# Expert stages in three chunks of groups inside one block, with tiles of 128 places

## Time and profile before

| what | value |
|---|---|
| median of 3 runs | 2091.97 us (2087.68 to 2100.49) |
| the profiled execution | 2083.64 us, span 2081.6 us |
| mean granted TensorE clock | 0.909 of 2.4 GHz |
| busy share of the span | PE 83%, PE weight loads 60%, DVE 60%, ACT 51%, POOL 42% |
| expert stages, from the last routing of attention to the field stage | about 264 to 756 us |

### The profile page before, as it was taken

How to read it: one execution, slowest core, us unless ns; L and a number is a source line. 1 busy time by engine, 2 the same in 40 slices (tenths; PEclk the granted TensorE clock), 3 DMA queues, 4 the chain that set the end, 5 groups by cost and what they waited for, 6 DMA issues and landing times. The chain is left out here.

```text
span 2081.6 us, 37284 instructions
## 1 busy us (share of the span) xinstructions
PE 1736.5 (83%) x12051; PEld 1241.9 (60%) x12051; DVE 1258.1 (60%) x3243; ACT 1067.8 (51%) x3158; POOL 873.5 (42%) x1095
## 2 busy tenths in 40 slices
PE   0899629974299849999868999999999999899887
PEld 0344429864198826556557677777777777555533
DVE  7587624536345378787667566655665665456556
ACT  0443204331143328788544566656666666666643
POOL 0246646546555513343318756070606060622233
PEclk9997659995599959999979999999999999999999
DMA  2920023322122250000023221212121212110001
GB/s 63 416 69 22 30 72 107 97 85 84 49 70 63 58 195 23 26 25 25 25 77 80 60 57 47 57 47 57 47 58 46 57 48 60 53 48 29 25 12 41
DMA packets 155838, 135.89 MB, mean 65 GB/s; under 512 B 87957, under 2 KB 128214, under 8 KB 153494
## 3 DMA queue, kind: packets, MB, share of 16 engines
q1 hardware_dynamic: 146582, 115.08, 18.9%
q0 software_dynamic: 9088, 18.70, 2.8%
HBM read 77.17 MB, written 56.54 MB: 64 GB/s over the span
## 5 line engine op out<-in xcount | busy, mean ns | idle before, releaser
L2676 DVE TENSOR_TENSOR delta_sv<-delta_sv,delta_zp 32x256 f32<-32x256 f32 x384 | 161.2, 420 | 168.4 <-PE delta_zp L2317 162.0
L818 POOL DMA_INDIRECT y<-moe_y,moe_aim x156 | 177.1, 1135 | 161.4 <-DVE moe_y L958 69.0
L2589 POOL TENSOR_TENSOR delta_dd<-delta_ll,delta_minus 128x1024 f32<-128x1024 f32 (+1 forms) x9 | 24.3, 2700 | 382.4 <-DMA delta_ll<-lanes 382.3
L1771 ACT ACTIVATE field_p<-field_sp,field_nm 128x128 f32<-128x128 f32 x512 | 179.9, 408 | 0.9 <-DVE field_nm L1855 0.8
L2596 POOL TENSOR_TENSOR delta_dd<-delta_dd,delta_prod 128x30 f32<-128x30 f32 (+11 forms) x270 | 151.4, 561 | 21.1
L2594 POOL TENSOR_TENSOR delta_prod<-delta_ll,delta_dd 128x30 f32<-128x30 f32 (+11 forms) x270 | 139.4, 516 | 21.2
L2317 PE MATMUL delta_zp<-delta_sv,delta_ct 128*32 128x128 f32 x1536 | 122.5, 281 | 20.1 <-DVE delta_sv L2676 12.4
L2285 PE MATMUL delta_xp<-delta_la,delta_di 128*128 128x256 f32 x512 | 121.4, 392 | 12.9 <-DMA delta_di<-inverses 7.0
L1771 ACT ACTIVATION_READ_ACCUMULATOR field_p<-field_sp,field_nm 128x1 f32 x512 | 127.6, 249 | 0.0
L2317 PEld LDWEIGHTS delta_zp<-delta_sv,delta_ct 128*32 128x32 f32 x1536 | 70.3, 110 | 85.0 <-DVE delta_sv L2676 50.7
L2285 PEld LDWEIGHTS delta_xp<-delta_la,delta_di 128*128 128x128 f32 x512 | 97.3, 194 | 37.6 <-issue 25.3
(11 more groups left out here) (564 smaller groups left out, 4554.3 us busy)
## 6 DMA issues: line engine op xcount, KB each, us to landing
delta_al<-alpha SPq DMA_DIRECT2D x33, 512.0 KB, 4.4
pairs<-c_none SPq DMA_DIRECT2D x16, 1032.0 KB, 16.3
moe_xg<-pairs SPq DMA_DIRECT2D x78, 129.0 KB, 2.2
moe_yt<-y SPq DMA_DIRECT2D x16, 512.0 KB, 4.5
w_E<-in_E_dram SPq DMA_DIRECT2D x1, 4624.0 KB, 36.9
w_E<-in_E_dram SPq DMA_DIRECT2D x8, 578.0 KB, 4.0
lanes<-delta_la SPq DMA_DIRECT2D x128, 32.0 KB, 1.7
delta_di<-inverses SPq DMA_DIRECT2D x64, 64.0 KB, 2.3
```

The source lines that it names most:

```text
L818: nc.gpsimd.indirect_dma_start(results, bass.IndirectOffsetOnAxis(ap=aim[:, t % AR, j:j + 1], axis=0), y[:, t % YS, j, :], None).then_inc( ...
L1771: last = nc.scalar.activation(p[:, slot, h, :], s_ps[i][:, k, :], ACT.Exp, bias=nm[:, slot, h:h + 1], accum_out=zs[:, slot, h:h + 1])
L2676: nc.vector.tensor_tensor(sv[rows, two, :], sv[rows, two, :], z_ps[2 * pair // HH][rows, at, :], ALU.subtract).then_inc(s["z_kept"], 1)
```

## The change

The groups are taken in three chunks: 0 to 2, 3 to 5, 6 and 7. Each chunk has its own regions in `pairs` and its own tiles: 31, 31 and 23, in all 85 tiles of 128 places in each of the two layers (39 of 256 before). Tiles of layer one run through all chunks, then those of layer two, in one block `experts` without a barrier between. While tiles run, the results of a chunk that is done are combined and routed again, in steps given by ROUTE_AT and FINISH_AT (the tile at which a group's first step is due; the next steps follow 1 to 6 tiles later).

- Results are no longer scattered by pair. SyncE stores each tile's rows in order (`store`), and GpSimd later fetches each token's two rows with indirect DMAs (`fetch`, 8 a group), by the places (`aim`) that `pair_weights` now also works out. The pair's number goes out of the rows, `valid` and `no_token` out of `tile_tables`.
- In `retention` only groups 0 to 3 are scattered; groups 4 to 7 at the start of `experts`. The tables of chunk 0 are made as soon as group 2 is placed.
- The transposes and the results have one PSUM bank each in place of two; the loads are 8 tiles ahead in place of 4.
- The weighing of one of the two results moves to ScalarE (4 activations a group), the rest is one operation for 128 tokens on VectorE (`mix`, 4 a group).
- The field basis is cut into steps among the tiles. E2 is loaded in eight parts during tiles 0 to 7 (before: every fourth tile).

The core of the diff (old functions `tiles_first`, `combine_first`, `tiles_second` and `combine_second` are taken out whole):

```
-SLOTS = 256
-TILES = 2 * B * T // SLOTS + NE - 1
-ROW = D + 1
+SLOTS = 128
+SUBS = SLOTS // 128
+CHUNKS = ((0, 3), (3, 6), (6, 8))
+CHUNK_TILES = [(last - first) * GT * 2 // SLOTS + NE - 1 for first, last in CHUNKS]
...
 retention, gpsimd:
-                for u in range(GROUPS + 4):
+                for u in range(GROUPS + 2):
...
-                        if 0 <= q < GROUPS:
-                            scatter(nc, pool, g, dram, q, b)
+                        if 0 <= q < PR:
+                            scatter(nc, pool, c, dram, q, b)
...
-                all_scattered(pool, g)
...
 retention, vector:
+                        if chunk_end(nc, ch, g, w, c, u - 3) == 0:
+                            ch.link(tile_tables(nc, ch, g, w, c, 0, 0))
...
-                tile_tables(nc, ch, g, w, c)
...
+ROUTE_AT = {128: (40, 45, 51, 72, 78, 83, 105, 111), 256: (24, 28, 32, 43, 47, 51, 59, 63)}[SLOTS]
+FINISH_AT = {128: (127, 133, 138, 156, 161, 167), 256: (77, 80, 83, 96, 99, 102)}[SLOTS]
...
+    H1, H2, XR, WR, YS, YR = 2, 4, 8, 5, 3, 3
...
 experts, sync:
+                for t in range(XR):
+                    load(t)
+                for t in range(2 * TILES):
+                    store(t)
+                    if t + XR < 2 * TILES:
+                        load(t + XR)
+                    if t < NE:
+                        sp.dma_start(w["E2"][:, t, :], E2[:, t, :]).then_inc(loaded_2, 16)
...
 experts, gpsimd:
+                for u in range(PR, GROUPS):
+                    for b in range(GB):
+                        scatter(nc, pool, c, dram, u, b)
+                nc.gpsimd.memset(none[:], 0.0).then_inc(primed, 1)
+                for k, (first, last) in enumerate(CHUNKS):
+                    all_stored(0, k)
+                    pool.wait_ge(aimed, k + 1)
+                    for u in range(first, last):
+                        fetch(u, 0, k)
+                    for u in range(first, last):
+                        pool.wait_ge(g["placed"], u + 1)
+                        for b in range(GB):
+                            scatter(nc, pool, c, dram, u, b)
+                for k, (first, last) in enumerate(CHUNKS):
+                    all_stored(1, k)
+                    pool.wait_ge(aimed, len(CHUNKS) + k + 1)
+                    for u in range(first, last):
+                        fetch(GROUPS + u, 1, k)
...
 experts, tensor:
+                def turn(t):
+                    pe.wait_ge(gathered[t % XR], 16 * (t // XR + 1))
+                    if t >= 1:
+                        pe.wait_ge(x_kept, t)
+                    for j in range(SUBS):
+                        last = nc.tensor.transpose(xT_ps[:, j * 128:(j + 1) * 128], xg[:, t % XR, j, :], w["ident"][:])
+                    last.then_inc(turned, 1)
...
+                def first_layer(t):
+                    pe.wait_ge(x_kept, t + 1)
+                    pe.wait_ge(staged, t + 1)
...
+                def third_layer(t):
+                    pe.wait_ge(h2_kept, H1 * (t + 1))
+                    if t >= 1:
+                        pe.wait_ge(y_kept, t)
...
+                def turn_rows(q):
+                    pe.wait_ge(mixed, q + 1)
+                    pe.wait_ge(turn_kept, q)
...
+                def logits(u):
+                    pe.wait_ge(turn_kept, u + 1)
...
+                def combine(step):
+                    for u in due(ROUTE_AT, step - 1):
+                        turn_rows(u)
+                    for u in due(ROUTE_AT, step - 2):
+                        logits(u)
+                    for u in due(ROUTE_AT, step - 4):
+                        gate_count(nc, pe, g, w, u, count_ps)
+                    for u in due(FINISH_AT, step - 1):
+                        turn_rows(GROUPS + u)
...
+                for s in range(-3, TILES):
+                    if s + 3 < TILES:
+                        turn(s + 3)
+                    if 0 <= s + 2 < TILES:
+                        first_layer(s + 2)
+                    if 0 <= s + 1 < TILES:
+                        second_layer(s + 1)
+                    if 0 <= s:
+                        third_layer(s)
+                        field_tensor(pe, s)
+                        combine(s)
+                for s in range(TILES - 2, 2 * TILES):
+                    if s + 2 < 2 * TILES:
+                        turn(s + 2)
+                    if TILES <= s + 1 < 2 * TILES:
+                        wide_layer(s + 1)
+                    if TILES <= s:
+                        last_layer(s)
+                        combine(s)
...
 experts, scalar, in combine(step): weigh at due(ROUTE_AT, step), keep_m (the copy of the
 transposed rows) at step - 2, gate_exp at step - 3, each behind the tile's activations
...
 experts, vector:
+                def keep_x(t):
+                    if 2 <= t < TILES + 2:
+                        dve.wait_ge(h1_made, H1 * (t - 1))
...
+                    dve.wait_ge(turned, t + 1)
+                    nc.vector.tensor_copy(xT[:, t % 2, :], xT_ps).then_inc(x_kept, 1)
...
+                def combine(step):
+                    for u in due(ROUTE_AT, step - 1):
+                        mix(u)
+                    for u in due(ROUTE_AT, step - 3):
+                        shift(u)
+                    for u in due(ROUTE_AT, step - 4):
+                        gate_pick(nc, dve, ch, g, c, u)
+                    for u in due(ROUTE_AT, step - 5):
+                        gate_place(nc, dve, ch, g, c, u, count_ps)
+                        k = chunk_end(nc, ch, g, w, c, u)
+                        if k is not None:
+                            tile_tables(nc, ch, g, w, c, 1, k).then_inc(tabled, 1)
+                            dve.wait_ge(tabled, len(CHUNKS) + k)
+                    for u in due(ROUTE_AT, step - 6):
+                        for k, (_, last) in enumerate(CHUNKS):
+                            if u + 1 == last:
+                                pair_weights(nc, ch, c, one, total, k).then_inc(aimed, 1)
+                    for u in due(FINISH_AT, step - 1):
+                        mix(GROUPS + u)
+                    for u in due(FINISH_AT, step - 2):
+                        residual(u)
...
+                for s in range(-4, TILES):
+                    if s + 4 < TILES:
+                        stage_weights(s + 4)
+                    if 0 <= s + 3 < TILES:
+                        keep_x(s + 3)
+                    if 0 <= s:
+                        keep_y(s)
+                        for k in range(1, len(CHUNKS)):
+                            if s == 2 * k - 1:
+                                tile_tables(nc, ch, g, w, c, 0, k).then_inc(tabled, 1)
+                                dve.wait_ge(tabled, k)
+                        for k in range(len(CHUNKS)):
+                            if s == 7 + 2 * k:
+                                pair_weights(nc, ch, c, one, total, k).then_inc(aimed, 1)
+                        field_vector(dve, s)
+                        combine(s)
+                for s in range(TILES - 3, 2 * TILES):
+                    if TILES <= s + 3 < 2 * TILES:
+                        stage_weights(s + 3)
+                    if TILES <= s + 2 < 2 * TILES:
+                        keep_x(s + 2)
+                    if TILES <= s:
+                        keep_y(s)
+                        combine(s)
+                for u in range(len(FINISH_AT), GROUPS):
+                    mix(GROUPS + u)
+                    residual(u)
```

More of the change, by code:

```diff
@@ L185, in tile_tables, with scatter @@
+def scatter(nc, pool, c, dram, n, b):
+    for k in range(2):
+        nc.gpsimd.indirect_dma_start(dram["pairs"], bass.IndirectOffsetOnAxis(ap=c["index"][:, n, k, b:b + 1], axis=0),
+                                     c["rows"][:, n % PR, b, :], None).then_inc(c["scattered"][n % PR], 16)
+def tile_tables(nc, ch, g, w, c, layer, k):
+    n = CHUNK_TILES[k]
+    shape = [128, n, NE]
     of_tile = lambda ap: ap.unsqueeze(1).to_broadcast(shape)
-    t = w["count"][:, 0:TILES]
-    ch.link(nc.vector.tensor_tensor(g["cnt"][:], g["behind"][:], w["region"][:], ALU.subtract))
@@ L213, in tile_tables @@
[L213 to L227 removed]
+    off = c["off"][:, k, :]
@@ L1004, in sync, with stored_all @@
         sp.dma_start(dram["fa"], e[:]).then_inc(stored, 16)
+    def stored_all(sp):
         sp.wait_ge(stored, 16)
[L1007 to L1016 removed]
@@ new lines, in last_layer @@
+                def last_layer(t):
+                    pe.wait_ge(y_kept, t)
+                    for j in range(SUBS):
+                        for k in range(H2):
+                            if j == 0:
+                                pe.wait_ge(h_kept, H2 * (t - TILES) + k + 1)
+                            last = nc.tensor.matmul(y_ps[:, j, :], hid[:, t % 2, k, j * 128:(j + 1) * 128], part(t, 512 + k * 128),
+                                                    start=(k == 0), stop=(k == H2 - 1))
+                    last.then_inc(y_made, 1)
@@ new lines, in wide_layer, with weigh @@
+                def wide_layer(t):
```

(27 more changed lines are left out.)

878 lines of the change are left out of this document (317 added, 561 removed).

## The result

The changed kernel took 2305.11 us (median of 4 runs, 2300.06 to 2322.26) against 2090.16 us for the kernel before (4 runs, 2087.68 to 2100.49): ratio 1.1025, 95% interval 1.0964 to 1.1087. It is slower, as forecast, but by 215 us where +82 was forecast (2172), and outside the forecast's range of 2055 to 2235. The profiled execution spans 2320.4 us (before 2081.6), at a clock of 0.883 (before 0.909).

What follows compares the result with a forecast made beforehand. It took tiles to be bound by TensorE, the rest by chains and GpSimd's scatter queue. 278 + 362 + 123 + 7 + 37 + 32 = 839 us to the field stage, +83 us, hence 2172, range 2055 to 2235.

Steps and rivals of the forecast that it cites:

- part 5: From last tile to field stage, 31.8 us against 32.9 before; GpSimd's DMAs elsewhere were said to set nothing.
- B, the clock: Rival: TensorE's clock stays low through all routing stretches, +43 us on the forecast, 2215; chance 0.14.
- Way in: End of attention to first finished tile: first load at 265.4 us, first tile kept at 278, against 310.3 before.
- Plain tile: One tile of 128 places without group work: 2.14 us, 169 of them 362 us.
- the loop: In the tiles, from keep_x through TensorE and keep_y to a later keep_x: 4.27 us over two tiles, 2.14 each.
- Rival A: Faster: the two-tile wait on keep_x doesn't bind, VectorE's queue alone sets 1.92 us a tile; 2056 us, chance 0.20.
- C: Rival: TensorE hides everything in the tiles, 1.89 us each and 30 us of extras; 1995 us, chance 0.05.
- E: Rival: weight loads come between short matmuls, not under them; 3.9 us a tile, 2470 us in all, chance 0.02.
- A routing group: Routing steps inside the tiles, eight groups: 7.1 us each on top of plain tiles, 57 us together.
- All extras and the clock: On top of plain tiles: 123 us routing and combining, 7 turn between layers, 37 for the fallen clock.
- Way out: Behind the last tile: 16 indirect fetches, weighing and adding, next block at 31.8 us, against 32.9 before.
- rival D: GpSimd's fetch costs 1.6 us, dearer than a scatter: some 25 us exposed, 2197 us, chance 0.09.

Runs made afterwards that it cites:

- e5_again: The changed kernel once more, nothing altered, in an occasion without stalls: 2142.89 us, ratio 1.0301 to the kernel before.
- occasions 2 and 1: Sets of kernels sent together on chip 13, without stalls: 2 held the changed kernel again (2142.9 us), 1 the changed kernel with 256 places (2160.9).
- the first four experiments: Changed kernel with a memset and wait behind each indirect DMA 2169.59 us, 8 result buffers 2142.47, plain DMAs for fetches 2125.07, tiles of 256 places 2160.89.
- e18_256: The changed kernel with tiles of 256 places instead of 128, in an occasion with stalls: 2306.74 us.
- e9_x_paced: The changed kernel with keep_x on ScalarE and a memset of 128x512 with a wait behind every indirect DMA of the block: 2139.93 us.
- e17_two_paced: Changed kernel with two chunks, keep_x on ScalarE, a 128x128 memset and wait behind the block's indirect DMAs except the last 32: 2103.22 us, 1.0036 of the kernel before.

## Why the prediction was wrong, and where it was right

**The step that failed** is the last of part 5: "GpSimd elsewhere: 224 DMAs x 1.26 = 282 us in over 500; the groups' due steps leave it several us of reserve each, so it sets nothing." It asked whether GpSimd would be in time, and it is (its own queue waits for others). It put at nothing what a row of its DMAs does to the engines beside it, and the trace of before has no case of it: beside tiles GpSimd has 75 instructions in 143.7 us, about two a tile, and beside its long row TensorE has no work at all (264 to 297); in attention its rows are of four, and of eight once, at 245.07, where TensorE works 4.3 of 10 us. The change put rows of 8 to 32 of them into the tile pipeline, and the stalls stand in those of 24 and 32. Shown: pausing between the DMAs takes the stalls away (2139.9 against 2265.6, same occasion), more buffers don't (2265.6 against 2264.3 without them, in another occasion with stalls). Not shown: whether it is the wider spacing or GpSimd's wait behind each DMA that helps, since the pause has both. The price of the stalls is 162 us by the medians of the changed kernel's two kinds of occasion; in the two traces the field stage starts 180 us apart. Not one of the five rivals held such a case; B, the clock, came nearest in kind, but the pause brings the time back without touching the tiles, so the low clock in those windows (0.58 to 0.69) goes with the stalls and doesn't make them.

**Without the stalls the forecast was 29 us high**: 2142.9 against 2172, inside its range (61 us over the kernel before in that occasion, where 80 to 83 were forecast). Part of that is luck, for terms on both sides were off. By its terms, in the trace of e5_again:
- Way in: first tile kept at 285.5, forecast 278 and outside its bounds, 275 to 281. The term that failed is chunk 0's tables in the middle of attention, priced at 2 us exposed (bounds 0 and 3.9). VectorE's index of group 2, just ahead of them, is written at 192.02 (192.05 before); that of group 3 at 224.85 (215.84 before), 9.0 us late, and the last one at 273.20 (263.85 before), 9.35 late. The tables themselves take VectorE from 192.50 to 196.96, and TensorE, which waits for its next operation, stands 4.75 us and then works at half clock (0.50 from 200 to 208, where before it was 1.00):

```profile
192.50 0.29 DVE L196 TENSOR_TENSOR ret_over<-c_cnt,w_steps 128x128 f32<-128x128 f32 x1
...
196.79 0.17 DVE L211 TENSOR_SCALAR c_where<-ret_where 1x31 int32<-1x31 f32 x1
...
200.41 2.09 PE L511 MATMUL ret_sp<-ret_qm,ret_kT 32*128 32x512 f32 x8 [4.75 <-DVE ret_pT L699]
```

  The block's end cost what was priced: VectorE acts 1.26 us after its last operation in retention, where 1.2 was taken. But the first load starts 1.05 behind that, at 275.75, which the sum leaves out. From first load to first tile it is 9.7 against 10.6.
- Plain tile: 2.14 forecast. In layer one keep_y stood at 362.32, 364.33, 366.73, 368.75 and 371.15, turns of 2.0 and 2.4, 2.21 on average; in layer two 16.56 us for eight (664.53 to 681.09), 2.07. With keep_x off VectorE a tile takes 1.89, which is TensorE's own time as counted, and 41 us go in 169 tiles, 0.24 each. So what bound the tile runs through keep_x on VectorE. That run shortens VectorE's own queue as well, but a queue of 1.92 alone doesn't give 2.14, and VectorE waits 0.39 for TensorE before keep_y in every second tile (362.32, 366.73). (By its own rows the loop is 4.22 us, not 4.27: 387.77 to 387.82 is 0.05, and 1.16 less four of 0.11 is 0.72. That makes 2.11 a tile.) Rival A (1.92 with keep_x on VectorE) and C fall; so does E, for eight matmuls and a transpose with their weight loads fit into 1.89. By the ratio of the two figures for matmuls of 128 columns, 81 ns with a weight load each and 56 alone (the Trainium skill, TensorE: Matmul & The Clock Gate, Back-to-back issue gap), a tile would take 2.7 us, an estimate; the trace doesn't agree, its tile takes 1.89.
- A routing group: 7.1 forecast. The first one stands between 399.78 and 417.73, five tiles: 17.95 less 5 x 2.14 is 7.25.

```profile
399.78 0.29 DVE L1234 TENSOR_TENSOR moe_y<-moe_bank,moe_wt 128x128 f32<-128x128 f32 x1
403.83 0.29 DVE L1234 TENSOR_TENSOR moe_y<-moe_bank,moe_wt 128x128 f32<-128x128 f32 x1 [1.50 <-PE moe_bank L1074]
...
407.65 0.29 DVE L1234 TENSOR_TENSOR moe_y<-moe_bank,moe_wt 128x128 f32<-128x128 f32 x1 [1.14 <-PE moe_bank L1074]
409.71 0.27 DVE L1234 TENSOR_TENSOR moe_y<-moe_bank,moe_wt 128x128 f32<-128x128 f32 x1
414.12 0.29 DVE L1234 TENSOR_TENSOR moe_y<-moe_bank,moe_wt 128x128 f32<-128x128 f32 x1 [1.16 <-PE moe_bank L1074]
417.73 0.28 DVE L1234 TENSOR_TENSOR moe_y<-moe_bank,moe_wt 128x128 f32<-128x128 f32 x1
```

- All extras and the clock: forecast 123 + 7 + 37 = 167 on top of 362. Measured 491.7 from first to last keep_y, so 130. The clock may be the term that was too large: it stood at 1.00 from 397 to 418, where group 0 is routed, and from 508 to 545, where two of the second chunk's groups are, and fell only later. But its fall was not priced in these stretches alone, so this is argued, not shown:

```profile
397.00:418.00 21.00, 14.59 (x123) 13.67 (x122) 12.43 (x54) 10.61 (x36) 13.72 (x13) 1.00 0.30 83
418.00:477.00 59.00, 40.73 (x258) 39.09 (x259) 32.52 (x135) 18.74 (x60) 23.49 (x23) 0.78 0.19 57
...
508.00:545.00 37.00, 24.17 (x201) 22.68 (x200) 19.59 (x96) 15.87 (x53) 13.94 (x15) 1.00 0.23 67
```

  How the 37 that the loop took less split between extras and clock was not measured. Rival B (43 more) is out.
- Way out: 31.8 forecast, 777.2 to 809.34 is 32.1. A fetch costs what a scatter does, 0.95 and 0.30 between, and beside tiles the rows of fetches start 1.30 to 1.42 us apart (rival D, 1.6 us, is out).

So 285.5 + 491.7 + 32.1 = 809.3, forecast 839: 7.5 late on the way in, 37 too much in the loop.

**Tiles of 128 places**, the other part of the change, can be judged too: where nothing stalls, 128 places are 18 us (0.8%) better than 256 in this program (2142.9 against 2160.9, occasions 2 and 1 of one chip); where it stalls they are level (2305.3 and 2306.7, in different occasions). With either the kernel stays above the one before. Two chunks with keep_x on ScalarE come down to a draw: 2080.4 against 2079.7, and with the pause, which held in both kinds of occasion, 0.4 to 0.7% over the kernel before. No version beat it.

**What stays open.** What in the chip is held up: TensorE's signals, or its matmuls themselves, whose ends the profile only models; no view shows which. What makes an occasion one with stalls. Whether spacing is what counts, and where its limit is: rows beside tiles at 1.26 to 1.35 us on average stall and rows at 1.63 to 1.75 don't, though these have single starts 1.44 apart. And whether the remote waits of ScalarE and keep_y have one cause or two; the pause removes both.

## What to carry to other kernels

Moving a queue of GpSimd's indirect DMAs beside a tight pipeline needs a price for what it does to the neighbours, not only for whether it is in time; if the trace of before never shows such a row beside busy engines, give that a rival of its own with a wide bound. Keep such DMAs a little apart: a memset of 128x128 and a wait behind each cost 12 us of 2080 where nothing was wrong, and nothing stalled with them in an occasion with stalls; a longer one saved 126 us in another. Work put in the middle of a busy stage isn't covered because it is short: 4.5 us of tables on VectorE made the stage 9 us longer. And when a result has long waits that end in nothing the profile names, run the unchanged program again, on another occasion, before explaining it: the first four experiments here told nothing of the stalls until that was done.

## What the runs showed of the hardware that was not expected

Beside rows of 24 or 32 indirect DMAs some 1.3 us apart, what TensorE hands to ScalarE and VectorE came late, with waits of up to 20.4 us in the first profile and 24.3 in e18_256, with the DMA engines at 18% to 30%; what VectorE's keep_x hands to TensorE did not (0.30 us at most in the first profile). Rows of 8 did little (5.3 us at most in the first profile). On other occasions, on chip 13 too, the same instructions delayed nothing. The program then differs by 7.6% (2305.3 against 2142.9) while the kernel before differs by 0.5% (2091.9 against 2081.8). And a memset of 128x512 on GpSimd takes 0.55 us by itself and 1.04 beside a weight copy of VectorE, one of 128x128 0.22 and 0.72; no memset without such a copy beside it is long, in e9_x_paced and e17_two_paced.
